# An adaLN block with a Mamba-2 scan: last weights staged in eight buffers, and the loads around them in another order

## The chip, the cores and the metric

One core of a Trainium2 chip runs the whole program. The metric is the device time of one execution in microseconds, lower is better. Everything is fp32; the large products are made of three TensorE passes over split operands (a high part in the reduced format fp32r and the low remainder).

## The reference, cut to what matters

```python
mod = (silu(c) @ wmod).reshape(4, 6, 1, 512)               # sa, ca, ga, sb, cb, gb
h = layernorm(x) * (1 + ca) + sa                            # x: 4 x 512 x 512
xBCzA = h @ in_proj_w.T                                     # x 1024, B 512, C 512, z 1024, A 64
xBC = silu(causal_depthwise_conv4(xBCzA[..., :2048]) + bias)
y = ssd_chunk_scan(x, -softplus(A), B, C, 128) + D * x / dt # 64 heads of 16, 8 groups of state 64
out = (y * silu(z + z_bias)) @ out_proj_w.T                 # 1024 -> 512
x = x + ga * out
h = layernorm(x) * (1 + cb) + sb
bw = where(w >= 0, 1, -1) * mean(|w|, axis=1)               # binarized ffn weight, 512 x 512
return x + gb * (h @ bw.T + b_ffn)
```

## The kernel before, in words

The program has three parts. A prologue makes the modulation, the normalized input `h_hi`/`h_lo` (4 batches, resident in SBUF) and the decays of all heads, which go to scratch tensors in DRAM. The main part and the tail follow in one block; each engine's instruction stream is written out by hand, and engines meet only at semaphores.

**The main part** has 16 steps (4 pairs of groups `gp` times 4 batches `b`), each of 4 units of 128 tokens, so 64 units, v = 0 to 63; every engine runs over v = -2 to 63, and a unit has four slots (`sl`). In a unit TensorE multiplies states and diagonal blocks (L1023, L1036, L1049), the Gram matrix (L1061), turns x and B (L1003, L1013), multiplies decays (L994) and makes one and a half tiles of the input projection, 12 matmuls of 128x512 each, for a step ahead (L985). ScalarE evicts the tiles, takes tanh and exp; VectorE makes the convolution taps (L1223), the silu (L1245, L1250), the product `mix` (L1259), `update` and `collect` (L1289, L1273, L1275); GpSimd makes the state decay and finishes y, step by step, in `t1`. The SP queue issues all DMAs in program order and waits itself: in each unit it waits until the decay product of unit v+2 is done, then loads the decays of unit v+4 (`R`, `Lm`); at the first unit of a step it first waits for GpSimd's y of the step before (L917), stores it (L918) and loads the scales `ea` (L893); at the third unit it loads the skips `dd`.

**Weights** come in raw, 128 rows of 512, are turned by TensorE in two pieces (`weights(i)`, L1074, a piece is 2 transposes; piece 2j is in slot 3 of a unit, piece 2j+1 in slot 0 of the next), evicted by ScalarE (L1166 to L1170), and their low part is made on GpSimd. Two raw buffers `wraw` alternate. For the next group pair, six blocks (pieces 0 to 11): blocks 0 and 1 are loaded at (b, i) = (0, 3), the others at (2, 0) to (2, 3), each behind what SP does in that unit; block 2 is turned in slot 3 of the group's unit 9, that is (2, 1). For the tail, twelve blocks j: 0 to 7 of the output projection, 8 to 11 of the ffn weight; block j is loaded by SP in unit 49+j (`OUT_UNIT` - 1 + j) and turned in units 50+j and 51+j. Before an ffn block is turned, ScalarE takes its absolute value (`magnitudes`, L1176, slot 3 of units 57 to 60), and VectorE its mean and its signs in place (`signs`, L1295 to L1302, slot 1 of units 58 to 61). `alpha` (L1084), a product of ones with the means, follows in unit 63.

**The tail** has 16 steps (batch, block of 128 rows), numbered n = 0 to 15. For each: y loaded from scratch (`load_tail_y`, 512 KB), x loaded (256 KB), ScalarE's `high_y` (L1523), GpSimd's `low_y` (L1562), 24 matmuls (L1683, `project`), `residual` on VectorE (L1613 to L1621: times gate `ga`, plus x, statistics), the reciprocal deviation on GpSimd (L1577 to L1581), `normalize` (L1532) on ScalarE, four transposes (L1698, `turn`), scale and shift (L1547, L1553), the low part (`split`, L1637), 8 matmuls (L1713, `linear`) and `finish` (L1650, L1653). Projections 0 and 1 already run in slots of units 61 to 63 (`TAIL_AT`). Project(n+2) needs low_y(n+2), which needs high_y(n+2), which stands behind normalize(n) on ScalarE. SP in unit 59 loads y of blocks 0, 1 and x of blocks 0 to 3; in unit 62 it waits for the last input projection and the last decay product, and then loads gates 0, the ffn bias, y of blocks 2, 3 and the other gates. GpSimd's `shift(b)` (L1572) multiplies the bias by gate `gb` of batch b: shift(0) before its tail starts, and shift(1) to shift(3) in steps 0 to 2; VectorE's `scale_gates(b)` (L1628) in steps 0 to 3. After unit 63 VectorE runs residual(0), then finishes the last y of the main part (L1336, L1339), which SP stores (`store_last`) before its later tail loads.

Of the kernel before, what the change touches and what calls it, by code (L numbers as in the profile page):

```python
# [10 lines left out]
P = 128  # L11
# [134 lines left out]
def early_tail(nc, s, ctx):  # L146
# [7 lines left out]
    s.y_hi, s.y_lo = sb("y_hi", [P, 2, DI // P, P], F32R), sb("y_lo", [P, 2, DI // P, P], F32R)  # L154
# [5 lines left out]
    s.d_gate, s.d_bias = [sem(f"d_gate{b}") for b in range(NB)], sem("d_bias")  # L160
# [625 lines left out]

TAIL_AT = {246: (0, 0), 247: (0, 1), 249: (0, 2), 250: (0, 3), 251: (1, 0), 253: (1, 1), 254: (1, 2), 255: (1, 3)}


def main_part(nc, s, outer, x, w_in, w_out, w_ffn, b_ffn):  # L790

    with ExitStack() as ctx:
# [47 lines left out]
        def chunk(u, c):  # L840
            first = (u % UPS) * U_TOK + c * Q
            return slice(first, first + Q)

# [23 lines left out]
        def sync(sp, tail):  # L867
# [41 lines left out]
            def load_last_weights(j):  # L909

                r, hh = j % 4, j // 4
                src = w_out[r * P:(r + 1) * P, hh * D:(hh + 1) * D] if hh < 2 else w_ffn[r * P:(r + 1) * P, :]
                sp.wait_ge(w_pe, NWP + 2 * (j - 2) + 2)
                sp.dma_start(wraw[:, j % 2, :], src).then_inc(wraw_ready[j % 2], 16)
# [12 lines left out]
            for v in range(-2, NU):  # L927
# [12 lines left out]
                if v >= 0 and n // NB < GP - 1:  # L940
# [4 lines left out]
                    if (b, i) in ((2, 0), (2, 1), (2, 2), (2, 3)):  # L945
                        load_weights(gp + 1, i + 2)

                if 0 <= v - OUT_UNIT + 1 < (NWO + NWF) // 2:
                    load_last_weights(v - OUT_UNIT + 1)
                if v == 59:  # L950
# [7 lines left out]
                if v == 62:  # L958

                    sp.wait_ge(in_done, len(TILES))  # L960
                    sp.wait_ge(d_done, 2 * NU)
                    load_gates(s, sp, 0)
                    sp.dma_start(s.bias, b_ffn.rearrange("(o n) -> o n", o=1).broadcast_to([P, D])).then_inc(s.d_bias, 16)
                    for t in range(2, 4):
                        load_tail_y(nc, s, sp, 0, t)
                    for b in range(1, NB):
                        load_gates(s, sp, b)
# [6 lines left out]
        def tensor(pe, tail):  # L974
# [90 lines left out]
            def weights(i):  # L1065

                raw, half = i // 2, i % 2
                if half == 0:
                    pe.wait_ge(wraw_ready[raw % 2], 16 * (raw // 2 + 1))
                    if i >= NWP + NWO:  # L1070
                        pe.wait_ge(s.w_sign, (i - NWP - NWO) // 2 + 1)
                wait(pe, w_copied, i)
                for k in range(2):
                    ins = pe.transpose(XT[:, k * P:(k + 1) * P], wraw[:, raw % 2, (2 * half + k) * P:(2 * half + k + 1) * P],  # L1074
                                       s.ident[:, :])
# [48 lines left out]
        def scalar(act, tail):  # L1124
# [47 lines left out]
            def magnitudes(r):  # L1172

                act.wait_ge(wraw_ready[r % 2], 16 * ((NWP + NWO) // 4 + r // 2 + 1))
# [585 lines left out]
```

## Time and profile before

| | |
|---|---|
| median of 3 runs | 780.71 us (777.64 to 781.13) |
| the profiled execution | 776.95 us, its span 775.1 us |
| mean granted TensorE clock | 0.929 of full speed |
| busy: TensorE, VectorE, ScalarE, GpSimd | 681.3, 523.3, 377.8, 384.4 us |
| DMA moved | 71.55 MB, mean 92 GB/s |

The profile records one execution. All times in rows are microseconds from the start of the span. 1.85 us of the profiled execution lie outside its span. "Idle before" is time in which an engine had nothing to run, and the name behind it is what ended that time; "issue" stands where the profile saw no engine that did, which is also what a wait for a DMA can look like on TensorE.

### The profile page before, as it was taken

The page shows a single profiled execution, that of the slowest core. Times are in us where ns is not written, and L with a number is a line of the kernel's source. Part 1 is how long each engine was busy: PE and PEld are TensorE (multiplying, and loading weights), DVE is VectorE, ACT ScalarE, POOL GpSimd, SP SyncE. Part 2 cuts the span into 40 slices and gives each one's busy share as a digit, 9 for nine tenths or more (in the row PEclk, how much of TensorE's full clock was granted, in tenths as well). Part 3 has the DMA queues.
Part 4 walks back from the last instruction along what each step waited for, and adds up shares of the span by engine and source line. Part 5 has one row for each costly group of instructions (what it writes and reads, how often), then busy time and mean ns, then how long its engine had stood idle before and what let it go on. Part 6 is the DMA issues. An engine that isn't in the chain of part 4 may idle for free. (4 is left out here: it accounts for less than half of the span.)

```text
span 775.1 us, 20785 instructions
## 1 busy us (share of the span) xinstructions
PE 681.3 (88%) x8194; PEld 533.1 (69%) x8194; DVE 523.3 (68%) x940; ACT 377.8 (49%) x812; POOL 384.4 (50%) x465
## 2 busy tenths in 40 slices
PE   6678348999989999989999989999875797999995
PEld 6457116777767777767777767777664575788883
DVE  2759576878857777758778777687572454665643
ACT  0562413455554644555554554655562425565653
POOL 2674800144535435446345364456471547776761
PEclk9666579999999999999999999999997799999998
DMA  7440352111132022123123123122322563535311
GB/s 199 110 163 28 135 189 60 35 60 63 62 98 77 33 88 89 33 94 107 35 68 108 34 86 98 53 74 75 112 88 61 166 163 124 155 117 156 118 41 41
DMA packets 61909, 71.55 MB, mean 92 GB/s; under 512 B 13992, under 2 KB 32936, under 8 KB 61812
## 3 DMA queue, kind: packets, MB, share of 16 engines
q1 hardware_dynamic: 56372, 70.17, 28.5%
q8 instruction: 66, 1.08, 0.6%
q10 hardware_dynamic: 5440, 0.05, 0.4%
q14 instruction: 31, 0.25, 0.1%
HBM read 54.45 MB, written 15.75 MB: 91 GB/s over the span
## 5 line engine op out<-in xcount | busy, mean ns | idle before, releaser
L1223 DVE SCALAR_TENSOR_TENSOR m_cv<-bank,gpc,m_cv 128x511 f32<-128x511 f32 (+2 forms) x192 | 143.6, 748 | 54.1 <-ACT m_cv L1132 49.5
L985 PE MATMUL bank<-h_hi,w_hi 128*128 128x512 f32 x384 | 159.1, 414 | 12.6 <-DVE m_Xp L1305 11.5
L985 PE MATMUL bank<-h_hi,w_lo 128*128 128x512 f32 x384 | 152.2, 396 | 0.0
L985 PE MATMUL bank<-h_lo,w_hi 128*128 128x512 f32 x384 | 151.6, 395 | 0.0
L1132 ACT ACTIVATE m_cv<-bank,gpc 128x512 f32<-128x512 f32 x96 | 71.9, 749 | 91.2 <-PE bank L985 91.2
L1358 POOL TENSOR_TENSOR m_S<-m_S,m_cd 128x128 f32<-128x128 f32 x96 | 39.8, 415 | 146.7 <-DVE m_S L1286 78.2
L985 PEld LDWEIGHTS bank<-h_hi,w_hi 128*128 128x128 f32 x384 | 73.3, 191 | 31.4 <-DVE m_Xp L1305 11.7
L1349 POOL TENSOR_TENSOR m_Xw<-m_Xp,wend 128x256 f32<-128x256 f32 x64 | 39.9, 624 | 110.1 <-ACT m_Xp L1152 110.1
L985 PEld LDWEIGHTS bank<-h_hi,w_lo 128*128 128x128 f32 x384 | 72.8, 190 | 16.9
L1144 ACT ACTIVATE m_M<-bank 128x512 f32<-128x512 f32 x128 | 76.3, 596 | 13.4 <-PE bank L994 11.8
L985 PEld LDWEIGHTS bank<-h_lo,w_hi 128*128 128x128 f32 x384 | 73.4, 191 | 13.7
L1259 DVE TENSOR_TENSOR m_M<-m_M,bank 128x512 f32<-128x512 f32 x128 | 81.7, 680 | 0.0
L1049 PE MATMUL pair<-m_M,m_Xp 64*32 64x64 f32 x4096 | 62.3, 229 | 0.0
L994 PE MATMUL bank<-R,Lm 84*128 84x512 f32 x128 | 58.3, 456 | 3.1 <-ACT m_M L1144 3.1
L1139 ACT ACTIVATE bank<-m_cv 128x512 f32<-128x512 f32 x96 | 58.1, 605 | 2.6 <-DVE m_cv L1223 2.6
L1250 DVE SCALAR_TENSOR_TENSOR m_gate<-bank,m_cv 128x512 f32<-128x512 f32 x32 | 22.1, 692 | 52.9 <-ACT bank L1139 52.9
L1683 PE MATMUL bank<-h_hi,t_y_hi 128*128 128x512 f32 x128 | 52.7, 411 | 3.3 <-POOL t_y_lo L1562 3.3
L1049 PEld LDWEIGHTS pair<-m_M,m_Xp 64*32 64x32 f32 x4096 | 54.6, 107 | 1.2 <-issue 0.2
L1683 PE MATMUL bank<-h_lo,t_y_hi 128*128 128x512 f32 x128 | 51.4, 402 | 0.0
L1683 PE MATMUL bank<-h_hi,t_y_lo 128*128 128x512 f32 x128 | 51.4, 401 | 0.0
L1562 POOL TENSOR_TENSOR t_y_lo<-h_lo_place,t_y_hi 128x1024 fp32r<-128x1024 f32 x16 | 38.2, 2386 | 26.3 <-ACT t_y_hi L1523 26.3
L1152 ACT ACTIVATE m_Xp<-bank 128x256 f32<-128x256 f32 x64 | 24.3, 380 | 49.0 <-PE bank L1003 49.0
(178 smaller groups left out, 1368.0 us busy)
## 6 DMA issues: line engine op xcount, KB each, us to landing
m_ea<-ea_scratch SPq DMA_DIRECT2D x32, 256.0 KB
m_dd<-dd_scratch SPq DMA_DIRECT2D x32, 256.0 KB
y_scratch<-m_t SPq DMA_DIRECT2D x16, 512.0 KB, 3.4
h_lo_place<-y_scratch SPq DMA_DIRECT2D x16, 512.0 KB, 4.3
p_wm<-in_L_wmod_dram SPq DMA_DIRECT2D x6, 1024.0 KB, 6.3
m_wraw<-in_L_attn_in_proj_w_dram SPq DMA_DIRECT2D x18, 256.0 KB, 3.3
p_xt<-in_L_attn_input__dram SPq DMA_DIRECT2D x16, 256.0 KB, 2.8
w_lo_place<-in_L_attn_input__dram SPq DMA_DIRECT2D x16, 256.0 KB, 4.5
```

Of the source, the lines that this page charges most:

```text
L985: ins = pe.matmul(A[k % 3][:, :], w[:, t, kc, :], h[:, n % NB, kc, :], start=(m == 0), stop=(m == 11))
L994: pe.matmul(DB[:, :], s.Lm[:, u % 2, q, :], s.R[:, u % 2, q, :], start=True, stop=True).then_inc(d_done, 1)
L1049: ins = pe.matmul(YS[32 * j:32 * j + 32, c, q * Q:(q + 1) * Q], Xp[half, u % 2, HG * q + h, :], M[half, u % 2, q, h * Q:(h + 1) * Q], star ...
L1132: act.activation(cv[:, k % 3, :], A[k % 3][:, :], ACT.Identity, scale=scale, bias=bias).then_inc(lin_done, 1)
L1139: act.activation(A[k % 3][:, :], cv[:, k % 3, :], ACT.Tanh).then_inc(tanh_done, 1)
L1144: act.activation(M[:, u % 2, q, :], DB[:, :], ACT.Exp).then_inc(exp_done, 1)
L1223: ins = dve.scalar_tensor_tensor(out=cv[:, k % 3, lag:], in0=A[k % 3][:, 0:L - lag], scalar=s.gpc[:, gp, o:o + 1], in1=cv[:, k % 3, lag:], ...
L1259: dve.tensor_tensor(m, m, g, ALU.mult).then_inc(m_done, 1)
L1349: pool.tensor_tensor(Xw[:, :, :].rearrange("p q (j e d) -> p (q j) e d", e=2, d=HD), src, w, ALU.mult).then_inc(xw_done, 1)
L1358: pool.tensor_tensor(S1[:, c, :].rearrange("p (h d) -> p h d", h=HG), S[:, (m - 1) % 4, :].rearrange("p (h d) -> p h d", h=HG), cd[:, gp, ...
L1562: pool.tensor_tensor(y_lo[:, st.b % 2, :, :], yt_v(st.b), y_hi[:, st.b % 2, :, :].bitcast(F32), ALU.subtract).then_inc(ylo_done, 1)
L1683: ins = pe.matmul(OB[i][:, :], y[:, i, k, :], w[k], start=(k == 0 and m == 0), stop=(k == KI - 1 and m == 2))
```

## The change

Two SBUF tensors of the tail, `y_hi` and `y_lo` (16 KB of each partition), are not used until unit 60. The change lays eight raw buffers `s.raw` in the same bytes. Blocks 0 to 9 of the last weights use them (block j in buffer (6+j) mod 8), blocks 10 and 11 use `wraw`. Each block has its own semaphore.

- Loads of last weights: blocks 0 to 7 in units 40 to 47, 10 and 11 in units 49 and 50 (after the last input weights are turned), 8 and 9 in units 53 and 54 (after blocks 0 and 1 are turned).
- `magnitudes` in slot 3 of units 55 to 58 (was 57 to 60), `signs` in slot 3 of units 56 to 59 (was slot 1 of 58 to 61). Block j is turned where it was.
- Input weights of the next group pair: blocks 2 to 5 loaded at (1, 3), (2, 0), (2, 1), (2, 2), each one unit earlier.
- First y tiles and x tiles in unit 58 (was 59). In unit 61 (was 62), behind the wait for the last projection alone: y 2, `ga` 0, y 3, bias; then, behind the wait for the last decay product, `gb` 0 and the other gates.
- residual(0) at slot 0 of unit 63, ahead of that unit's `collect`; the last y (`close`) behind residual(1). `shift(b+1)` and `scale_gates(b)` in the third step of each batch. GpSimd waits in unit 61 until block 9 is turned.

```diff
-    s.y_hi, s.y_lo = sb("y_hi", [P, 2, DI // P, P], F32R), sb("y_lo", [P, 2, DI // P, P], F32R)
+    with nc.sbuf_tensor("t_y_hi", [P, 2, DI // P, P], F32R) as s.y_hi, nc.sbuf_tensor("t_y_lo", [P, 2, DI // P, P], F32R) as s.y_lo:
+        pass
+    s.raw = sb("raw", [P, 8, D])
+    s.raw_ready = [sem(f"raw_ready{j}") for j in range((NWO + NWF) // 2)]
...
+SIGN_AT = {55: 0, 56: 1, 57: 2, 58: 3}
+LAST_WEIGHTS_AT = {**{40 + j: j for j in range(8)}, 49: 10, 50: 11, 53: 8, 54: 9}
...
+        def raw_of(j):
+
+            if j < NWO // 2 + 2:
+                return s.raw[:, (6 + j) % 8, :]
+            return wraw[:, j % 2, :]
...
-                src = w_out[r * P:(r + 1) * P, hh * D:(hh + 1) * D] if hh < 2 else w_ffn[r * P:(r + 1) * P, :]
-                sp.wait_ge(w_pe, NWP + 2 * (j - 2) + 2)
-                sp.dma_start(wraw[:, j % 2, :], src).then_inc(wraw_ready[j % 2], 16)
+                if hh < 2:
+                    src = w_out[r * P:(r + 1) * P, hh * D:(hh + 1) * D]
+                else:
+                    src = w_ffn[r * P:(r + 1) * P, :]
+                    sp.wait_ge(w_pe, NWP + 4 if r < 2 else NWP)
+                sp.dma_start(raw_of(j), src).then_inc(s.raw_ready[j], 16)
...
-                    if (b, i) in ((2, 0), (2, 1), (2, 2), (2, 3)):
-                        load_weights(gp + 1, i + 2)
-
-                if 0 <= v - OUT_UNIT + 1 < (NWO + NWF) // 2:
-                    load_last_weights(v - OUT_UNIT + 1)
-                if v == 59:
+                    if (b, i) in ((1, 3), (2, 0), (2, 1), (2, 2)):
+                        load_weights(gp + 1, 2 + (i + 1) % 4)
+
+                if v in LAST_WEIGHTS_AT:
+                    load_last_weights(LAST_WEIGHTS_AT[v])
+                if v == 58:
...
-                if v == 62:
+                if v == 61:
 
                     sp.wait_ge(in_done, len(TILES))
-                    sp.wait_ge(d_done, 2 * NU)
-                    load_gates(s, sp, 0)
+                    load_tail_y(nc, s, sp, 0, 2)
+                    load_gate(s, sp, 0, 0)
+                    load_tail_y(nc, s, sp, 0, 3)
                     sp.dma_start(s.bias, b_ffn.rearrange("(o n) -> o n", o=1).broadcast_to([P, D])).then_inc(s.d_bias, 16)
-                    for t in range(2, 4):
-                        load_tail_y(nc, s, sp, 0, t)
-                    for b in range(1, NB):
-                        load_gates(s, sp, b)
+            sp.wait_ge(d_done, 2 * NU)
+            load_gate(s, sp, 1, 0)
+            for b in range(1, NB):
+                load_gate(s, sp, 0, b)
+                load_gate(s, sp, 1, b)
...
-                act.wait_ge(wraw_ready[r % 2], 16 * ((NWP + NWO) // 4 + r // 2 + 1))
+                act.wait_ge(s.raw_ready[NWO // 2 + r], 16)
                 wait(act, s.w_stats, r)
-                act.activation(s.wabs, wraw[:, r % 2, :], ACT.Abs).then_inc(s.w_abs, 1)
+                act.activation(s.wabs, raw_of(NWO // 2 + r), ACT.Abs).then_inc(s.w_abs, 1)
...
-                    r = v - OUT_UNIT - NWO // 2
-                    if sl == 1 and 0 <= r < 4:
-                        signs(r)
-            tail.residual(dve, Step(0, 0))
+                    if sl == 3 and v - 1 in SIGN_AT:
+                        signs(SIGN_AT[v - 1])
+                    if (v, sl) == (NU - 1, 0):
+                        tail.residual(dve, Step(0, 0))
+
+        def close(dve):
+
...
                 if v in (60, 61):
+                    if v == 61:
+                        pool.wait_ge(w_pe, NWP + NWO + 4)
                     tail.low_y(pool, Step(0, v - 60))
...
+def load_gate(s, sp, g, b):
+
+    sp.dma_start((s.ga, s.gb)[g][:, b, :], s.g_d[g, b:b + 1, :].broadcast_to([P, D])).then_inc((s.d_ga, s.d_gb)[g][b], 16)
...
-            if st.gp == 0 and st.b < NB - 1:
-                shift(st.b + 1)
+            if st.b == 2 and st.gp < NB - 1:
+                shift(st.gp + 1)
...
-            if st.gp == 0:
-                scale_gates(st.b)
+            if st.n(1, 0) == 1:
+                main.close(dve)
+            if st.b == 2:
+                scale_gates(st.gp)
```

## Rows read from the trace of the kernel before

**Rows 1.** Who waited for whom, whole span: total us, times, longest

```profile
ACT t_att L1176 <- DMA m_wraw<-in_L_ffn_weight_dram: 16.9, 4, 7.0
...
PE bank L1074 <- issue: 15.6, 5, 4.8
```

**Rows 2.** Timeline of TensorE: start, length, instruction, idle time before it

```profile
218.12 0.64 PE L1074 MATMUL bank<-ident,m_wraw 128*128 128x128 f32 x2 [2.90 <-issue]
...
221.84 0.48 PE L985 MATMUL bank<-h_hi,w_hi 128*128 128x512 f32 x1
...
339.15 0.41 PE L1074 MATMUL bank<-ident,m_wraw 128*128 128x128 f32 x2 [3.07 <-issue]
...
341.50 0.47 PE L985 MATMUL bank<-h_hi,w_hi 128*128 128x512 f32 x1
...
551.88 0.78 PE L985 MATMUL bank<-h_hi,w_hi 128*128 128x512 f32 x1
...
583.26 0.66 PE L1074 MATMUL bank<-ident,m_wraw 128*128 128x128 f32 x2 [4.78 <-issue]
```

**Rows 3.** Timeline of the SP queue, first unit of a step

```profile
330.83 0.39 SPq L918 DMA_DIRECT2D y_scratch<-m_t  x1
...
334.91 0.36 SPq L907 DMA_DIRECT2D m_wraw<-in_L_attn_in_proj_w_dram  x1
```

**Rows 4.** Timeline of TensorE, first instruction of units 56, 57, 59, 60, 61 and 62

```profile
565.09 0.39 PE L1023 MATMUL pair<-m_Ct,m_S 128*128 128x128 f32 x2
...
572.36 0.61 PE L1023 MATMUL pair<-m_Ct,m_S 128*128 128x128 f32 x4
...
591.36 0.61 PE L1023 MATMUL pair<-m_Ct,m_S 128*128 128x128 f32 x4
...
605.75 0.64 PE L1023 MATMUL pair<-m_Ct,m_S 128*128 128x128 f32 x2
...
615.05 0.61 PE L1023 MATMUL pair<-m_Ct,m_S 128*128 128x128 f32 x4
...
626.80 0.61 PE L1023 MATMUL pair<-m_Ct,m_S 128*128 128x128 f32 x4
```

**Rows 5.** Timeline of VectorE, units 57, 58 and 63

```profile
575.80 1.28 DVE L1259 TENSOR_TENSOR m_M<-m_M,bank 128x512 f32<-128x512 f32 x2
...
587.41 0.69 DVE L1295 BATCH_NORM_STATS2 t_wsta<-t_att 128x6 f32<-128x512 f32 x1
...
589.51 1.27 DVE L1259 TENSOR_TENSOR m_M<-m_M,bank 128x512 f32<-128x512 f32 x2
...
635.41 0.68 DVE L1613 TENSOR_TENSOR t_att<-bank,w_hi_place 128x512 f32<-128x512 f32 x1
```

**Rows 6.** Timeline of ScalarE, start of the tail

```profile
637.07 0.60 ACT L1210 ACTIVATE w_hi_place<-bank 128x512 f32<-128x512 f32 x1 [7.51 <-PE bank L1084]
641.07 0.81 ACT L1532 ACTIVATE t_xn<-t_x,t_small 128x512 f32<-128x512 f32 x1 [3.40 <-POOL t_small L1581]
```

**Rows 7.** Timeline of TensorE, start of the tail

```profile
645.31 0.80 PE L1683 MATMUL bank<-h_hi,t_y_hi 128*128 128x512 f32 x1 [2.72 <-POOL t_y_lo L1562]
...
652.33 0.60 PE L1698 MATMUL bank<-ident,t_xn 128*128 128x128 f32 x4
...
654.61 0.39 PE L1683 MATMUL bank<-h_hi,t_y_hi 128*128 128x512 f32 x1
...
660.22 0.60 PE L1698 MATMUL bank<-ident,t_xn 128*128 128x128 f32 x4
```

**Rows 8.** Timeline of GpSimd, the two first steps of the tail

```profile
637.85 1.12 POOL L1577 TENSOR_TENSOR t_small<-t_small 128x1 f32<-128x1 f32 x1 [3.45 <-DVE t_small L1621]
...
647.70 0.18 POOL L1577 TENSOR_TENSOR t_small<-t_small 128x1 f32<-128x1 f32 x1
```

**Rows 9.** Instructions of L1428, the loads of y: time from issue to landing

```profile
DMA to landing us min/median/max: 4.1/4.3/9.9
```

More of the change, by code:

```diff
@@ L159, in early_tail @@
     s.d_x = [sem(f"d_x{t}") for t in range(4)]
-    s.d_gate, s.d_bias = [sem(f"d_gate{b}") for b in range(NB)], sem("d_bias")
+    s.d_ga, s.d_gb, s.d_bias = [sem(f"d_ga{b}") for b in range(NB)], [sem(f"d_gb{b}") for b in range(NB)], sem("d_bias")
     s.w_abs, s.w_stats, s.w_mean, s.w_diag, s.w_step, s.w_sign, s.al_pe, s.al_done = (
@@ L1067, in weights @@
                 raw, half = i // 2, i % 2
+                src = wraw[:, raw % 2, :] if i < NWP else raw_of(raw - NWP // 2)
                 if half == 0:
-                    pe.wait_ge(wraw_ready[raw % 2], 16 * (raw // 2 + 1))
-                    if i >= NWP + NWO:
+                    if i < NWP:
+                        pe.wait_ge(wraw_ready[raw % 2], 16 * (raw // 2 + 1))
+                    elif i < NWP + NWO:
+                        pe.wait_ge(s.raw_ready[raw - NWP // 2], 16)
+                    else:
                         pe.wait_ge(s.w_sign, (i - NWP - NWO) // 2 + 1)
@@ L1073, in weights @@
                 for k in range(2):
-                    ins = pe.transpose(XT[:, k * P:(k + 1) * P], wraw[:, raw % 2, (2 * half + k) * P:(2 * half + k + 1) * P],
-                                       s.ident[:, :])
+                    ins = pe.transpose(XT[:, k * P:(k + 1) * P], src[:, (2 * half + k) * P:(2 * half + k + 1) * P], s.ident[:, :])
                 ins.then_inc(w_pe, 1)
@@ L1202, in scalar @@
                         tanh(k)
-                    r = v - OUT_UNIT + 1 - NWO // 2
-                    if sl == 3 and 0 <= r < 4:
-                        magnitudes(r)
+                    if sl == 3 and v in SIGN_AT:
+                        magnitudes(SIGN_AT[v])
                     if (v, sl) in ((60, 0), (61, 0)):
@@ L1291, in signs @@
             def signs(r):
-                raw = wraw[:, r % 2, :]
+                raw = raw_of(NWO // 2 + r)
                 dve.wait_ge(s.w_abs, r + 1)
@@ L1417, in gpsimd @@
                 if v in (60, 61):
+                    if v == 61:
+                        pool.wait_ge(w_pe, NWP + NWO + 4)
                     tail.low_y(pool, Step(0, v - 60))
-        m_.store_last = store_last
+        m_.store_last, m_.close = store_last, close
         m_.sync, m_.tensor, m_.scalar, m_.vector, m_.gpsimd = sync, tensor, scalar, vector, gpsimd
@@ L1428, in load_tail_y @@
     sp.dma_start(s.yt[t].rearrange("p a (k n) -> p (a k) n", n=P), y_v[b, t]).then_inc(s.d_y[t], 16)
-def load_gates(s, sp, b):
-    sp.dma_start(s.ga[:, b, :], s.g_d[0, b:b + 1, :].broadcast_to([P, D])).then_inc(s.d_gate[b], 16)
-    sp.dma_start(s.gb[:, b, :], s.g_d[1, b:b + 1, :].broadcast_to([P, D])).then_inc(s.d_gate[b], 16)
+def load_gate(s, sp, g, b):
+    sp.dma_start((s.ga, s.gb)[g][:, b, :], s.g_d[g, b:b + 1, :].broadcast_to([P, D])).then_inc((s.d_ga, s.d_gb)[g][b], 16)
 def load_tail_x(nc, s, sp, x, b, t):
@@ L1566, in shift @@
         def shift(b):
-            pool.wait_ge(s.d_gate[b], 32)
+            pool.wait_ge(s.d_gb[b], 16)
             if b == 0:
@@ L1608, in residual @@
         dve.wait_ge(s.d_x[st.b], st.gp * 16 + 16)
-        dve.wait_ge(s.d_gate[st.gp], 32)
+        dve.wait_ge(s.d_ga[st.gp], 16)
         if st.n(1, 0) == 1:
```

## The prediction

> **What bounds the kernel now.** TensorE is busy for 88% of the span, so I first looked for the time in which it is not, by listing who waited for whom over the whole span. Two rows stand out that belong to the same thing: TensorE waited five times, 15.6 us in all, in front of the turning of raw weights, and ScalarE four times, 16.9 us, for the raw ffn weights themselves [rows 1]. I then read TensorE's timeline around each of the five. Outside of them the main part shows next to no gap on TensorE, so a microsecond taken from one of these waits is a microsecond of the whole; a wait of another engine counts only where TensorE stands behind it.
>
> The waits have one shape. At the first unit of a step SP stands until GpSimd has the last step's y, and only behind that store and the scales and decays does it issue the next weight block: stored at 330.83, weights at 334.91 [rows 3], while TensorE was ready for them some 3.1 us before 339.15 [rows 2]. So the block landed 4.2 us after its issue, and TensorE had stood since 336. This repeats once per group pair and twice in the output weights. A second cost follows some of them: behind an idle stretch the granted clock drops from 2.4 to 1.2 GHz and the same instructions take longer. From the turning to the next projection matmul it is 2.35 us at full clock (339.15 to 341.50) and 3.72 us at 218.12 to 221.84 [rows 2], a loss of 1.4 us. The turning at 583.26 took 0.66 instead of 0.41 us, and the matmul at 551.88 took 0.78 instead of 0.47 [rows 2]: two more such losses.
>
> **Part 1: input weights a unit earlier.** Nothing is added; three of the five waits are of this kind. The load now comes in the unit ahead of the store, when SP has just issued the decays, and waits only until the buffer's last piece is turned, in slot 0 of the next unit, some two microseconds later. It is then issued about 10 us earlier than at 334.91, and needs 4.2. The block behind it takes its old place at 334.9, and is turned a unit (7.27 us, 565.09 to 572.36 [rows 4]) later than the first: at least 3 us in hand. What stands behind SP's new wait are the next scales and store, which wait for GpSimd anyway. The fourth wait is the output block of the first step's unit 52; its new load is 9 units ahead.
> These four are worth 15.6 - 4.78 = 10.8 us [rows 1, 2] and two clock losses, 1.4 and (less, since only its end was slow) 1.2: **13.4 us**. Bounds: 10.8 if the clock losses came anyway; 0 if another wait stood right behind. TensorE's near gapless work elsewhere speaks against the latter.
>
> **Part 2: units 57 to 61.** Here the fifth wait (4.78 us at 583.26) is followed by ScalarE's waits for ffn blocks, the longest 7.0 us [rows 1], during which it can't evict the pieces that TensorE waits for. I cost this by units.
> - Unit 58 starts 4.78 earlier and has no slow clock, 1.4 less. But `signs` is now in units 56 and 57, which have convolutions. One takes 2.1 us of VectorE (587.41 to 589.51), and `mix` at 575.80 shows no idle time ahead of it, so it moves to 577.9 and ends at 579.2 [rows 5]. Behind it a silu (an estimate of 1.3, two halves of about half a `mix`) and 0.69 of statistics reach 581.2, and `magnitudes` of the next block waits for them, 0.6, then the copies of the turned piece, 0.6: 582.4. TensorE wants that at 583.26 - 4.78 + 2.15 = 580.6 (the second piece is turned 0.2 ahead of the projection, so 2.35 - 0.2 behind the first). So a new wait of 1.8; I take 1.5, since one `signs` without contention is nearer to 1.7. Bounds 0 and 4.2 (two full `signs`). Unit 59 starts 4.7 us earlier.
> - Unit 59 took 14.39 us (591.36 to 605.75) [rows 4]. It has no projection. Unit 56 has 18 matmuls of the kind of which 24 take 5.61 us (654.61 to 660.22 [rows 7]), 4.2 in all, which leaves TensorE 3.0 us of other work: the lower bound. The upper one is 14.39 - 7.0 = 7.4. Between them VectorE decides: 2.1 of `signs`, 1.3 of `mix` and, an estimate, 2.0 of updates, collect and one silu, 5.4 us. That saves 9.0.
> - Units 60 and 61 have 18 such matmuls as unit 56 has, and took 9.30 and 11.75 us [rows 4]. At 7.4 each they save 1.9 and 4.35. The last ffn block and the y tiles (loaded a unit earlier) are then there in time.
>
> Sum: 4.7 + 9.0 + 1.9 + 4.35 = **20.0 us**, with bounds of 15.3 and 22.4. The loads themselves, twelve of 0.4 us on SP and 256 KB each, cost nothing: they lie beside units in which SP waits for TensorE. GpSimd's new wait in unit 61 is for a piece turned in unit 60, so nothing too.
>
> **Part 3: start of the tail.** residual(0) ran at 635.41 [rows 5], though its projection was done some 3.5 us before. Now it is ahead of `collect`. What is late next is ScalarE, which stands at the copy of `alpha` until 637.67, so normalize(0) moves from 641.07 to 637.7 [rows 6]. From there to project(2) is 4.24 us as before (645.31 [rows 7]), through high_y and low_y: 641.9, 3.4 earlier. Its 24 matmuls took 7.02 us at the slow clock against 5.61 later [rows 7]; 1.4 more, if the shorter gap leaves the clock alone. Project(3) is then ready at 649.8, but its low_y waits for the reciprocal of step 1 on GpSimd, normalize and high_y; I estimate 650.5 for it, twice the 4.24 us behind 641.9. It was at 654.61. I take **4.3 us**, bounds 0 and 4.8. The gates: `ga` 0 is issued about 3 us earlier than before. In a queue as full as this a 512 KB load took up to 9.9 us [rows 9]; with that residual(0) would come at 633, still early. Where `bias` or `gb` 0 are as late, GpSimd's shift(0) holds the reciprocal and part 3 loses up to all. The shifts and scalings that are spread over the batches are the same work and lie beside TensorE's.
>
> `close` now stands behind residual(1), beside GpSimd's small operations of step 1 instead of step 0. Beside it the first of them took 1.12 us in step 0, and 0.18 in step 1 [rows 8]. The Trainium skill, "GPSIMD Engine Reference", section Specifications, says that GpSimd's SBUF interfaces are shared with VectorE and contend with its instructions of two SBUF inputs, which `close` has. By that rule project(3) comes 0.9 us later than without contention and part 3 gives 3.4, by the row's place in step 0 alone it gives 4.3.
>
> **The sum.** 13.4 + 20.0 + 4.3 = 37.7 us. The profiled execution took 776.95, so it would take 739.2. The median of the runs is 780.71, 3.8 us above it, so I predict 780.7 - 37.7 = **743 us**. About 0.5% (4 us) is what this measurement can tell from no change.
>
> **Rivals.**
> - *The wait moves to VectorE (0.15).* `signs`, `magnitudes` and the next `signs` wait for each other in turn, and each stands in a unit of the full schedule. For it: no idle time ahead of `mix` [rows 5]. Against it: unit 58 has no convolution to come. If each of the three later ones costs its 2.1 us on TensorE, that is 6.3, and one clock loss of 1.4: 751 us.
> - *The tail's start gains nothing (0.10).* Bias and gate 0 land late, or project(2) and (3) wait for GpSimd as before. For it: the DMA queue is full there and a load took 9.9 us [rows 9]. 743 + 4.3 = 747 us.
> - *The change doesn't do what it says in the input weights (0.05).* If what TensorE waited for was not the load (the row says "issue" and names no DMA), or a new wait on SP takes its place, 13.4 us stay: 756 us. Against it: the landing time of 4.2 us fits.
> - *Contention of VectorE and GpSimd (0.05).* The second instance of it delays project(3) by 0.9: 744 us.
> - *Slower than before (0.02).* The decays stand in the same queue as the weights. They are issued nearly two units, some 14 us, before their use. If weight blocks ahead of them held them longer than that, TensorE would wait in each of some 24 units with such a load. To be slower than 784 it must eat 41.6 us, 1.7 a unit, so landing would have to take 16 us; the longest seen is 9.9 [rows 9].
>
> **The numbers.** My case as summed has 0.60, and for itself 738 to 748. With the first two rivals and the contention that is 0.90; something smaller that I don't see has 0.03 either way. The range of 736 to 755 leaves out the third and fifth rival and half of the unseen. Faster by over 0.5% in all cases but the last and the worst of the unseen: 0.96; within 0.5% 0.02; slower 0.02.
>
> **What would show it.** Right: no wait over 1 us in front of L1074; no row of L1176 waiting for a DMA; unit 59 under 7 us; project(2) within 2.5 us behind turn(0); a clock near 0.94 or above. Wrong: a wait of TensorE for L1166 to L1170 behind L1176 waiting for L1295 (first rival); L1572 waiting for a DMA past 634 less the shift (second); L1074 still at "issue" (third); L994 waiting (fifth).

## The result, and the profile after

The changed kernel takes 748.07 us (median of 4 runs, 746.02 to 748.24) where the kernel before takes 780.92 (median of 4, 777.64 to 781.92): ratio 0.9607, 95% interval 0.9578 to 0.9635 (recorded from the single runs; the two medians alone would give 0.958). The prediction was 743 us, range 736 to 755. The profiled execution took 748.24 us, its span is 746.5 and the mean granted clock 0.944 (before: 776.95, 775.1 and 0.929). Span against span the change gives 28.6 us, where the steps of the prediction promised 37.7.

The page of the profile after: busy times of the engines, TensorE in 40 slices, and its granted clock in the same slices.

```profile
PE 674.1 (90%) x8194; PEld 527.1 (71%) x8194; DVE 536.5 (72%) x940; ACT 376.5 (50%) x812; POOL 389.4 (52%) x465
...
PE   6679256899999999999999999999998999999995
...
PEclk9757577999999999999999999999999999999997
```

From the eighth slice to the last but one TensorE is at 80% or more. Its busy time was 681.3 us before; the same number of instructions now takes 7 us less, which fits the higher mean clock.

Who waited for whom after, whole span:

```profile
PE bank L1707 <- POOL t_y_lo L1584: 7.0, 5, 1.5
...
PEld bank L1094 <- issue: 5.7, 28, 0.4
```

And one row of the same list of the kernel before:

```profile
PE bank L1683 <- POOL t_y_lo L1562: 3.3, 2, 2.7
```

The five waits in front of the turning of raw weights [rows 1] are gone (L1094 is L1074 of before), and so is ScalarE's wait for the ffn blocks. One row has grown: TensorE waits five times, 7.0 us in all, for `low_y` of GpSimd (L1584, before L1562) in the tail, where it waited twice, 3.3 us, before. The waits at project(2) and (5) were there before, with 2.72 and 0.63 us; they are 1.52 and 1.38 now, and those at project(3), (9) and (13) are new.

Busy times after in units 56 to 61, cut at the starts of the units, which answer to [rows 4]. Columns: stretch, its length, busy us (and instructions) of TensorE, weight loads, VectorE, ScalarE and GpSimd, granted clock, DMA share, GB/s:

```profile
552.27:560.01 7.74, 7.50 (x119) 5.75 (x118) 5.61 (x12) 5.80 (x14) 4.08 (x6) 1.00 0.01 4
560.01:568.11 8.10, 5.42 (x109) 4.04 (x108) 7.96 (x16) 4.78 (x12) 4.79 (x8) 0.98 0.42 131
568.11:575.34 7.23, 7.23 (x106) 5.62 (x106) 7.09 (x14) 3.78 (x10) 4.64 (x6) 0.78 0.06 12
575.34:581.06 5.72, 4.08 (x103) 2.86 (x102) 4.63 (x13) 3.65 (x10) 1.61 (x4) 1.00 0.42 130
581.06:589.79 8.73, 8.42 (x120) 6.69 (x118) 5.08 (x12) 4.27 (x10) 7.00 (x8) 0.80 0.75 227
589.79:597.23 7.44, 7.44 (x122) 6.03 (x121) 3.27 (x8) 5.41 (x12) 4.64 (x6) 1.00 0.53 161
```

Unit 59, which took 14.39 us, takes 5.72. In unit 57 VectorE is full (7.96 of 8.10) and TensorE is not; units 58 and 60 run in part at the slow clock, 0.78 and 0.80.

The same view in four stretches, cut at the starts of units 56 and 62, turn(1) and turn(15):

```profile
552.27:597.23 44.96, 40.09 (x669) 30.98 (x668) 33.63 (x71) 27.68 (x63) 26.76 (x34) 0.92 0.38 114
597.23:617.98 20.75, 19.23 (x221) 14.90 (x219) 13.05 (x19) 6.43 (x15) 12.71 (x13) 1.00 0.61 185
617.98:733.62 115.64, 107.08 (x482) 84.41 (x481) 77.32 (x102) 63.83 (x139) 86.32 (x73) 1.00 0.36 109
733.62:746.50 12.88, 6.69 (x20) 4.59 (x20) 3.37 (x5) 2.90 (x8) 0.32 (x1) 0.69 0.11 41
```

The same four stretches of the kernel before:

```profile
565.09:626.80 61.71, 43.89 (x668) 33.27 (x667) 30.33 (x71) 27.91 (x63) 27.84 (x35) 0.81 0.33 99
626.80:652.33 25.53, 20.71 (x222) 15.99 (x221) 12.17 (x21) 7.34 (x15) 13.88 (x14) 0.93 0.77 214
652.33:761.56 109.23, 105.53 (x481) 84.98 (x480) 66.81 (x100) 63.47 (x138) 79.50 (x72) 1.00 0.35 107
761.56:775.10 13.54, 7.40 (x20) 5.18 (x20) 3.37 (x5) 2.90 (x8) 0.33 (x1) 0.75 0.10 39
```

The whole difference lies in these rows. Unit 1 of the main part started at 143.14 before and at 144.36 after, in a prologue that the change does not touch; over all kernels below it lay between 142.3 and 145.0, so the first 1 or 2 us of any difference here mean nothing. I therefore count from there.

| stretch | before | after | difference | foretold |
|---|---|---|---|---|
| prologue, to unit 1 | 143.14 | 144.36 | +1.2 | 0 |
| unit 1 to unit 56 | 421.95 | 407.91 | -14.0 | -13.4 |
| unit 56 to unit 62 | 61.71 | 44.96 | -16.75 | -20.0 |
| unit 62 to turn(1) | 25.53 | 20.75 | -4.8 | -4.3 (to the whole tail) |
| turn(1) to turn(15) | 109.23 | 115.64 | +6.4 | 0 |
| turn(15) to the end | 13.54 | 12.88 | -0.7 | 0 |
| sum | 775.1 | 746.5 | -28.6 | -37.7 |

The fifth line is the surprise. The turns of `xn` in the tail came every 7.9 us before, but for 7.98 and 8.8 at turn(3) and turn(4). (From turn(0) to turn(1) it was 10.4 us, which is in the line above.) After, TensorE's timeline at projections 3, 5 and 9:

```profile
621.86 0.50 PE L1707 MATMUL bank<-h_hi,t_y_hi 128*128 128x512 f32 x1 [1.37 <-POOL t_y_lo L1584]
...
639.38 0.50 PE L1707 MATMUL bank<-h_hi,t_y_hi 128*128 128x512 f32 x1 [1.38 <-POOL t_y_lo L1584]
...
672.97 0.51 PE L1707 MATMUL bank<-h_hi,t_y_hi 128*128 128x512 f32 x1 [1.38 <-POOL t_y_lo L1584]
```

The first comes behind `close`; the others, with a like one at 706.57, behind the shifts of steps 2, 6 and 10. A step with such a wait takes 9.6 us, and the step ahead of the two last ones 8.2.

### The profile page after: what moved, and what is told of

The parts are those of the page before. It is cut to its first block and busy times, and to the rows that moved or that the text cites. A ratio compares the mean times of both kernels' runs of the same rounds, so it can differ in the third digit from the quotient of the medians.

```text
span 746.5 us, 20781 instructions
## 1 busy us (share of the span) xinstructions
PE 674.1 (90%) x8194; PEld 527.1 (71%) x8194; DVE 536.5 (72%) x940; ACT 376.5 (50%) x812; POOL 389.4 (52%) x465
## 3 DMA queue, kind: packets, MB, share of 16 engines
q8 instruction: 65, 1.06, 0.6%
## 5 line engine op out<-in xcount | busy, mean ns | idle before, releaser
L1379 POOL TENSOR_TENSOR m_S<-m_S,m_cd 128x128 f32<-128x128 f32 x96 | 39.7, 414 | 141.0 <-DVE m_S L1304 71.4
L1584 POOL TENSOR_TENSOR t_y_lo<-h_lo_place,t_y_hi 128x1024 fp32r<-128x1024 f32 x16 | 40.1, 2504 | 27.3 <-ACT t_y_hi L1545 27.3
```

The source lines that it names most:

```text
L1379: pool.tensor_tensor(S1[:, c, :].rearrange("p (h d) -> p h d", h=HG), S[:, (m - 1) % 4, :].rearrange("p (h d) -> p h d", h=HG), cd[:, gp, ...
L1584: pool.tensor_tensor(y_lo[:, st.b % 2, :, :], yt_v(st.b), y_hi[:, st.b % 2, :, :].bitcast(F32), ALU.subtract).then_inc(ylo_done, 1)
```

## The experiments

All ratios are to the kernel before, timed beside it on the same chip. "Units" is unit 56 to unit 62, "tail" is unit 62 to turn(15), both from the profiled execution, one for each kernel.

| kernel | median us | ratio, 95% interval | units | tail |
|---|---|---|---|---|
| before | 780.92 | 1 | 61.71 | 134.76 |
| after | 748.07 | 0.9607 (0.9578 to 0.9635) | 44.96 | 136.39 |
| 1 input weights only | 765.34 | 0.9851 (0.9821 to 0.988) | 59.71 | 134.76 |
| 2 shifts back | 745.99 | 0.9611 (0.958 to 0.9642) | 44.97 | 133.15 |
| 3 `close` back | 748.59 | 0.9631 (0.9591 to 0.967) | 45.04 | 135.08 |
| 4 shift ahead of low_y | 743.42 | 0.9572 (0.9543 to 0.9602) | 44.97 | 131.37 |
| 5 3 and 4 together | 741.6 | 0.9535 (0.9503 to 0.9567) | 44.83 | 130.18 |
| 6 and the sum ahead | 739.99 | 0.952 (0.9485 to 0.9556) | 45.03 | 129.70 |
| 7 signs as before | 748.47 | 0.9624 (0.9589 to 0.9659) | 44.13 | 136.39 |
| 8 signs one unit later | 746.19 | 0.9599 (0.9567 to 0.9631) | 42.77 | 136.42 |
| 9 6 and 8 together | 738.97 | 0.949 (0.9464 to 0.9515) | 41.94 | 129.64 |
| 10 9, y ahead of skips | 739.83 | 0.9501 (0.9475 to 0.9527) | 41.51 | 129.71 |
| 11 residual(0) back | 750.21 | 0.9635 (0.9606 to 0.9665) | 44.81 | 138.23 |

Among the kernels with the early loads a stretch that the edit does not touch repeats within 0.25 us (units 44.81 to 45.04, tail 136.39 to 136.42), so the two right columns tell apart what the whole times cannot. That does not hold where TensorE waits for late loads: experiment 1 changes nothing in units 56 to 61, and they took 59.71 us there and 61.71 in the kernel before, 1.2 of the 2.0 in unit 59. The gain of that stretch is thus known to 2 us only. The kernel before was timed anew three times, with medians of 776.94 (beside 1 to 4), 778.17 (5 to 8) and 778.65 us (9 to 11).

**1. Input weights only**, on the kernel before.

```diff
-                    if (b, i) in ((2, 0), (2, 1), (2, 2), (2, 3)):
-                        load_weights(gp + 1, i + 2)
+                    if (b, i) in ((1, 3), (2, 0), (2, 1), (2, 2)):
+                        load_weights(gp + 1, 2 + (i + 1) % 4)
```

> The kernel before, with input weight blocks 2 to 5 loaded one unit earlier and nothing else changed. Theory of the prediction: the three waits of 2.90, 3.07 and 2.47 us are for these loads, one with a clock loss of 1.4: 9.8 us faster than before, near 771. Rival: part of the gain of the first four waits comes from elsewhere, or a new wait on SP's w_pe takes some back: less than 7 us.

Measured: ratio 0.9851, a gain of 1.5% with the whole interval below 1, and unit 50 starts 10.3 us earlier, counted from unit 1. The waits for which nothing was changed are still there (L1074 of before, TensorE's timeline):

```profile
539.36 0.41 PE L1074 MATMUL bank<-ident,m_wraw 128*128 128x128 f32 x2 [2.56 <-issue]
...
573.89 0.66 PE L1074 MATMUL bank<-ident,m_wraw 128*128 128x128 f32 x2 [4.59 <-issue]
```

So three of the five rows named "issue" were the late load, as read from its landing time, and nothing took their place. The output block's wait (2.56 here) and the 4.59 of the last stage belong to the last weights. The third rival of the prediction, that it was not these loads, has fallen.

**2. Shifts and scalings back** in the first steps.

```diff
-            if st.b == 2 and st.gp < NB - 1:
-                shift(st.gp + 1)
+            if st.gp == 0 and st.b < NB - 1:
+                shift(st.b + 1)
...
-            if st.b == 2:
-                scale_gates(st.gp)
+            if st.gp == 0:
+                scale_gates(st.b)
```

> The changed kernel, with shift(1) to shift(3) back in steps 0 to 2 and scale_gates(0) to (3) back in steps 0 to 3. In the changed kernel turn follows turn in the tail after 7.9 us, but after 9.6 us in the steps behind each shift (627.58 to 635.51 is 7.9, 635.51 to 645.11 is 9.6), and TensorE waits there 1.38 us for low_y. Theory A: a shift (1.3 us) lengthens GpSimd's chain (reciprocal, low_y, sum), on which TensorE stands; three shifts spread cost 3 x 1.7 = 5.1 us, three in a row while the chain is still filling cost some 3 us, so this kernel is 2 to 3 us faster than the changed one (near 745.5) and has no 9.6 us step behind step 5. Rival B: the shifts are beside TensorE's work as predicted, and the 9.6 us steps come from something else (loads of the next batch): the steps stay and the time is 748. Rival C: the early gates land late and this waits at the start: slower than 748 by more than 2.

Measured: from step 5 on every step takes 7.9 us again; the first four take 9.38, 9.13, 8.37 and 8.81. Unit 62 to turn(1) is longer, 22.3 instead of 20.75 us, turn(1) to turn(15) shorter, 110.9 instead of 115.6. Together the tail is 3.2 us shorter than after. Spreading the shifts and scalings was thus a loss of 3.2 us, net of what it spares at the start; the ratio of the whole (0.9611) is too coarse to show it beside after's.

**3. `close` back**, ahead of residual(1).

```diff
+            if st.n(1, 0) == 1:
+                main.close(dve)
             if not is_first(st):
                 residual(dve, st)
...
-            if st.n(1, 0) == 1:
-                main.close(dve)
```

> The changed kernel, with the last y (close) ahead of residual(1) again. In the changed kernel the two small operations of GpSimd in step 1 took 1.17 and 1.60 us beside close (0.19 and 0.57 in step 0), and TensorE waited 1.37 us for low_y(3) at 621.86. Contention theory: beside step 0, where ScalarE stands at the copy of alpha anyway, they cost nothing; project(3) comes 1.4 to 1.7 us earlier, time near 746.5. Rival: low_y(3) is late for another reason (its own chain), then it stays at 621.9 or residual(1), now behind close, makes it later: 748 or above.

Measured: the second step takes 7.9 instead of 9.6 us and the tail 1.3 us less. GpSimd's first two operations of step 1, after and then here (its timeline; L1599 and L1601 work on one element per partition):

```profile
613.86 1.17 POOL L1599 TENSOR_TENSOR t_small<-t_small 128x1 f32<-128x1 f32 x1
615.11 1.60 POOL L1601 TENSOR_TENSOR t_small<-t_small 128x1 f32<-128x1 f32 x1
```

```profile
614.77 0.64 POOL L1599 TENSOR_TENSOR t_small<-t_small 128x1 f32<-128x1 f32 x1
615.49 0.55 POOL L1601 TENSOR_TENSOR t_small<-t_small 128x1 f32<-128x1 f32 x1
```

After, VectorE ran `close` from 613.62 to 616.3, over both of them. They took 2.8 us, here 1.2. The contention rival of the prediction is what happens, and larger than the 0.9 us given for it. The tail gains less than the 1.7 us of the second step, since the step to turn(3) takes 8.35 us here and 7.93 after. The Trainium skill, "GPSIMD Engine Reference", section Specifications, says that GpSimd's SBUF interfaces contend with VectorE's instructions of two SBUF inputs. These numbers agree: both instructions of `close` have two such inputs. No run changes only the number of inputs, so the rule itself is not tested here.

**4. The shift ahead of low_y**, in the same steps as in the change.

```diff
+            if st.b == 2 and st.gp < NB - 1:
+                shift(st.gp + 1)
             if two_more(st):
                 low_y(pool, st.next().next())
...
-            if st.b == 2 and st.gp < NB - 1:
-                shift(st.gp + 1)
```

> The changed kernel, with shift(b+1) in the same step (the third of a batch) but ahead of low_y instead of behind the sum. GpSimd is idle for 1.88 us there in each step, while ScalarE runs normalize and high_y. Theory A (chain): the 1.3 us of a shift go into that idle time, the three 9.6 us steps become 7.9, and the kernel is 4.5 to 5.5 us faster than the changed one, near 743. Rival B (work beside VectorE's is what costs, wherever it stands) or a late high_y: the steps stay near 9.6 and the time is 748.

Measured: the three steps of 9.6 us behind a shift are down to 7.9, that of `close` stays, and the tail is 5.0 us shorter, ratio 0.9572. The same instructions run, only their order differs. This experiment shows the mechanism best, by its stretches; its interval still overlaps after's. GpSimd's timeline of a step with a shift, after:

```profile
627.31 2.41 POOL L1584 TENSOR_TENSOR t_y_lo<-h_lo_place,t_y_hi 128x1024 fp32r<-128x1024 f32 x1 [1.88 <-ACT t_y_hi L1545]
629.67 1.75 POOL L1614 TENSOR_TENSOR t_f<-t_x,t_gbias 128x512 f32<-128x512 f32 x1
631.38 1.31 POOL L1594 TENSOR_TENSOR t_gbias<-gb,w_hi_place 128x512 f32<-128x512 f32 x1
632.65 0.64 POOL L1599 TENSOR_TENSOR t_small<-t_small 128x1 f32<-128x1 f32 x1
633.37 0.88 POOL L1601 TENSOR_TENSOR t_small<-t_small 128x1 f32<-128x1 f32 x1
634.35 0.26 POOL L1603 TENSOR_SCALAR t_small<-t_small 128x1 f32<-128x1 f32 x1
636.49 2.84 POOL L1584 TENSOR_TENSOR t_y_lo<-h_lo_place,t_y_hi 128x1024 fp32r<-128x1024 f32 x1 [1.88 <-ACT t_y_hi L1545]
```

and with the shift ahead:

```profile
624.60 1.31 POOL L1594 TENSOR_TENSOR t_gbias<-gb,w_hi_place 128x512 f32<-128x512 f32 x1
626.51 2.39 POOL L1584 TENSOR_TENSOR t_y_lo<-h_lo_place,t_y_hi 128x1024 fp32r<-128x1024 f32 x1 [0.60 <-ACT t_y_hi L1545]
628.86 1.75 POOL L1616 TENSOR_TENSOR t_f<-t_x,t_gbias 128x512 f32<-128x512 f32 x1
630.57 0.19 POOL L1599 TENSOR_TENSOR t_small<-t_small 128x1 f32<-128x1 f32 x1
...
634.28 2.41 POOL L1584 TENSOR_TENSOR t_y_lo<-h_lo_place,t_y_hi 128x1024 fp32r<-128x1024 f32 x1 [1.88 <-ACT t_y_hi L1545]
```

Without a shift one low_y follows the last by 7.77 us (626.51 to 634.28). In that loop GpSimd works 5.9 us and waits 1.88 for normalize and high_y, which ScalarE can only begin when GpSimd's reciprocal is there. TensorE's step is 7.90. The loop has 0.13 us of room in each step, so a shift of 1.31 us put between two low_y eats what ten steps save, and with the slower small operations behind it the loop took 9.18 (627.31 to 636.49). The low_y at its end also took 2.84 us instead of 2.41, which makes the 9.6 us from one projection to the next. In the 1.88 us in which GpSimd waits anyway, it costs nothing.

**5. Both**, `close` back and the shift ahead.

> The changed kernel with both edits of the tail that took a wait away: shift(b+1) ahead of low_y, and close ahead of residual(1). If they act on different waits (the three behind shifts, 1.7 each, and the one behind close, 1.3), they add up: turns 7.9 us apart throughout, 6 to 6.5 us below the changed kernel. If the wait behind close only moves the point from which GpSimd's chain is late, less than 5.5.

Measured: tail 130.18, that is 6.2 us less than after; the single edits gave 1.3 and 5.0. They add up. Ratio 0.9535, whose interval lies wholly below after's. The tail now is 4.6 us below before's, close to the 4.3 foretold for part 3.

**6. The sum too.** The addition of the shift (L1614 of after), which stood between low_y and the next reciprocal, goes ahead of low_y, and the shift behind low_y.

```diff
+            pool.tensor_tensor(f1[:, st.b % 2, :], x2[:, st.b, :], gbias[:, st.gp, :], ALU.add).then_inc(res_done, 1)
             if two_more(st):
                 low_y(pool, st.next().next())
+            if st.b == 2 and st.gp < NB - 1:
+                shift(st.gp + 1)
```

> As the kernel with close and shift moved, but here the sum x2 + gbias (1.3 to 1.75 us) stands ahead of low_y, in the 1.88 us in which GpSimd waits for high_y, and the shift behind low_y. Chain theory: GpSimd's chain is shortened by up to 1.7 us in every step, so the shift behind low_y costs nothing either, and also the small waits of 0.3 us go: as the kernel with close and shift moved or up to 1 us less. Rival: the sum waits for finish of two steps before, and delays low_y: waits of 0.5 us and more in each step, 5 us more.

Measured: the tail is 0.5 us shorter (129.70), all its steps take 7.9 to 8.2 us. GpSimd waits there 0.62 us for high_y and 1.58 for VectorE's statistics, so its work now leaves room in the loop, and a step with a shift behind low_y takes 8.1 us at most. The ratio, 0.952, cannot be told from that of 5.

**7 and 8. Where `signs` stand.** First in the units of before, slot 1; then in slot 3, one unit later than in the change.

```diff
-SIGN_AT = {55: 0, 56: 1, 57: 2, 58: 3}
+SIGN_AT = {57: 0, 58: 1, 59: 2, 60: 3}
...
-                    if sl == 3 and v - 1 in SIGN_AT:
+                    if sl == 1 and v - 1 in SIGN_AT:
```

```diff
-SIGN_AT = {55: 0, 56: 1, 57: 2, 58: 3}
+SIGN_AT = {56: 0, 57: 1, 58: 2, 59: 3}
```

> The changed kernel, with the early loads but magnitudes and signs where they were before (slot 3 of units 57 to 60, slot 1 of units 58 to 61). In the changed kernel units 56 and 57 last 7.74 and 8.10 us (7.27 for unit 56 before), with waits of TensorE of 1.08 and 1.59 us in unit 57 and a slow clock behind them. Theory S: the signs among the convolutions cause them; here units 56 and 57 take 7.3 and about 6.6, the block's copy waits nowhere for a load, units 58 to 61 grow by at most 1 in all, and the time is 2 to 3 us below the changed kernel. Rival: the light units 58 to 61 then carry signs in line with magnitudes and the copy of the piece, and lose as much as 56 and 57 gain: time as the changed kernel within 1.

> The changed kernel, with magnitudes and signs one unit later (slot 3 of units 56 to 59 and of 57 to 60). Theory S: unit 56 is back at 7.3 (0.45 less); unit 57 still has the signs behind its silu, so part of its waits stays, and signs(0) is used for the piece in slot 3 of unit 58 in time: 1 to 2 us below the changed kernel. Rival: TensorE now waits for the signs themselves in slot 3 of units 58 to 61, as block and signs are one unit apart: no faster or slower by up to 2.

Measured, units 56 to 61, one by one:

| | 56 | 57 | 58 | 59 | 60 | 61 | sum |
|---|---|---|---|---|---|---|---|
| before | 7.27 | 11.36 | 7.64 | 14.39 | 9.30 | 11.75 | 61.71 |
| after | 7.74 | 8.10 | 7.23 | 5.72 | 8.73 | 7.44 | 44.96 |
| 7 as before | 7.28 | 6.18 | 6.70 | 7.72 | 7.90 | 8.35 | 44.13 |
| 8 one later | 7.26 | 6.17 | 7.30 | 5.79 | 8.82 | 7.43 | 42.77 |

With the signs where they were, units 56 to 58 take 20.16 us, 6.1 less than before, all three at a clock of 1.00: the 4.78 + 1.4 that the prediction gave the load alone. After, they take 23.07, so the signs among the convolutions cost 2.9 us, where I had taken 1.5. But as before they make units 59 and 61 longer, with TensorE waiting 1.92 us for `mix` at 579.88, so the rival is nearer to what came. The wait of 1.08 us in unit 57, which the expectation gave to the signs, is not theirs: it is there in 7 and 8 too, and with 1.09 in the kernel before. One unit later is best: 2.2 us less than after. The whole times of 7 and 8 do not differ from after's by more than their intervals.

**9. Best of these**, 6 with the signs of 8.

> The kernel with close and the sum moved, and with magnitudes and signs one unit later. Units 56 to 61 took 44.96 us in the changed kernel and 42.77 with the signs one unit later; the tail's moves took 6.7 to 7.5 us out between turn(1) and turn(15). Theory: the two lie in different stretches and add up, 8.9 to 9.7 us below the changed kernel, near 738.5. Rival: the earlier start of unit 62 meets gates and y tiles that are not there, and the start of the tail gives it back: near 740.5.

Measured: units 41.94, tail 129.64, together 9.8 us less than after: the two add up. The ratio is 0.949, and its interval (0.9464 to 0.9515) lies below after's, so it beats both kernels. Its median is 39.7 us below the kernel before's.

**10. y ahead of the skips.** In unit 58 the loads of y 0 and 1 are issued before the skips.

> As the kernel before it in this set, with the two first y tiles issued in unit 58 ahead of the skips (two loads of 256 KB) instead of behind them. ScalarE waited 1.73 us for the first y tile in unit 60 of the changed kernel, and TensorE 1.2 us behind that with the signs later, with a slow clock after it. Theory: the tile comes 1.2 us and more earlier, unit 60 goes from 8.8 to at most 7.6 us, time 1 us or a little more below. Rival: the wait before it, for the last projection of step 14, sets the issue, and the skips come late for GpSimd: no gain.

Measured: unit 60 takes 7.52 instead of 7.95 us; the time of the whole shows no gain, as the rival said. ScalarE's wait for y 0 is thus real and, here, small.

**11. residual(0) back** behind the unit loop, all else as after.

```diff
-                    if (v, sl) == (NU - 1, 0):
-                        tail.residual(dve, Step(0, 0))
...
+            tail.residual(dve, Step(0, 0))
+
         def close(dve):
```

> The changed kernel with residual(0) behind unit 63 as before. Theory of the prediction: residual(0) starts 2.9 us later (605.3 instead of 602.4), but ScalarE stands at the copy of alpha until 608.1 anyway, so normalize(0) and project(2) come only 1.2 to 1.5 us later, 1.2 to 2.5 us above the changed kernel with the clock. Rival: the whole gain of 4.8 us at turn(1) hangs on this move, then turn(1) comes 3.5 to 5 us later.

Measured: turn(1) comes 24.0 us behind unit 62 (after 20.75, before 25.53), but it then waits for nothing at project(3), so the tail as a whole is 1.8 us longer than after's. ScalarE's timeline here:

```profile
607.07 0.60 ACT L1228 ACTIVATE w_hi_place<-bank 128x512 f32<-128x512 f32 x1 [7.52 <-PE bank L1103]
609.08 0.81 ACT L1553 ACTIVATE t_xn<-t_x,t_small 128x512 f32<-128x512 f32 x1 [1.42 <-POOL t_small L1602]
```

xn starts 2.0 us behind the copy of `alpha`. Before, it was 4.0 [rows 6], with residual(0) at the same place. What differs is that `close` no longer stands beside GpSimd's reciprocal of step 0: its three operations took 1.12, 1.62 and 0.27 us before, 3.0 in all, and here 0.19, 0.57 and 0.27. After, xn(0) follows the copy at once, at 608.00, as the prediction had it.

Experiment 3 is the other half of this comparison: residual(0) moved, and `close` beside step 0 as before. ScalarE's timeline there:

```profile
608.42 0.60 ACT L1228 ACTIVATE w_hi_place<-bank 128x512 f32<-128x512 f32 x1 [7.52 <-PE bank L1103]
608.91 0.81 ACT L1554 ACTIVATE t_xn<-t_x,t_small 128x512 f32<-128x512 f32 x1
```

| from unit 62 to | xn(0) | turn(1) |
|---|---|---|
| before | 14.3 | 25.5 |
| only `close` moved (11) | 12.3 | 24.0 |
| only residual(0) moved (3) | 10.8 | 20.7 |
| both (after) | 10.8 | 20.75 |

So residual(0) alone gives the whole 3.5 us at xn(0) and 4.8 at turn(1), as the prediction had it: the reciprocal is then done before the copy of `alpha` ends, contention or not. The move of `close` gives 2.0 only where residual(0) is late. With residual(0) moved too, it gives nothing at the start and costs 1.3 in the tail (experiment 3). The expectation's 1.2 to 2.5 us for the whole came true (1.8 in the tail), but turn(1) came 3.3 us later, nearly what its rival said.

## Why the prediction was right, and where it was not

The signs that the prediction named for being right all came: no wait over 1 us in front of L1094, no wait of L1195 (before L1176) for a DMA, unit 59 at 5.72 us, project(2) 2.1 us behind turn(0), a clock of 0.944. They test the loads and the start of the tail, and none of them looks at the tail's later steps, where it went wrong.

**Part 1, 13.4 us: 14.0.** The four waits and both clock losses are gone and nothing stood behind them; experiment 1 shows three of them alone (10.3, where their share of the sum was 9.8). No wait of TensorE took their place: L1094 shows none above 0.4 us.

**Part 2, 20.0 us: 16.75** (14.75 against the trace of experiment 1, which has the same late loads). The loads are what it hung on, and two of the four terms are right: unit 59 gave 8.7 (9.0 foretold) and unit 61 4.3 (4.35). The two others were mis-sized. (The bounds given for the part, 15.3 and 22.4, do not follow from those of its terms, which add up to 15.2 and 23.8.)
- To the start of unit 59: 3.2 instead of 4.7. I priced the signs among convolutions at 1.5, experiment 7 measures 2.9. The wait is where the prediction put it. TensorE's timeline at the end of unit 57:

```profile
567.60 0.33 PE L1029 MATMUL bank<-ident,m_Bt 128*128 128x128 f32 x1 [1.59 <-DVE m_M L1277]
567.76 0.55 PE L1094 MATMUL bank<-ident,t_raw 128*128 128x128 f32 x2
568.11 1.06 PE L1039 MATMUL pair<-m_Ct,m_S 128*128 128x128 f32 x4
```

  The 1.59 is the new wait for `mix`. What I had left out is behind it: the last row took 1.06 us where its kind takes 0.61, and the granted clock is 0.50 from 568.1 to 570.0: the short wait also brought slow clock. And one `signs` took 2.8 us, not 2.1, since its in-place step at 560.86 took 1.55 us beside a GpSimd multiplication, where it had taken 0.83.
- Unit 60: 0.6 instead of 1.9. TensorE is busy there for 8.42 of 8.73 us at a clock of 0.80: it is slow clock again, behind the light unit 59. Kernels in which unit 60 ran at a clock of 1.00 show a second cost that lay hidden under it: in 8 ScalarE stood 2.43 us for y 0 and TensorE 1.22 us behind it (8.82 us in all), in 9 it was 1.57 and 0.36 (7.95), in 10, with y issued earlier, 1.14 and none (7.52). So the 7.4 that I gave the unit is about what it takes with neither.

**Part 3, 4.3 us: a loss of 1.6**, outside its bounds of 0 and 4.8. Its start was as foretold: 4.8 us at turn(1), by the move of residual(0) (experiments 3 and 11). **The step that failed is the sentence that the spread shifts and scalings "are the same work and lie beside TensorE's".** They lie beside TensorE's work, but not beside GpSimd's own loop, and that is as long as TensorE's. The place of the shifts cost 5.0 us, 1.7 for each (experiment 4), the contention behind `close` 1.3 (experiment 3). Before, shift(1) and shift(2) stood where project(2) and (3) were late anyway, and shift(3) cost about 0.9 there: the step to turn(4) took 8.8 us.

The steps of 8.2 us stay in experiments 4 and 5 and are gone in 2. No run moves the scalings alone, but the traces point at them. VectorE's timeline after, ahead of such a step, and then GpSimd's:

```profile
656.07 0.84 DVE L1650 TENSOR_TENSOR gb<-gb,w_hi_place 128x512 f32<-128x512 f32 x1
...
657.67 0.69 DVE L1675 TENSOR_TENSOR t_o<-t_o,t_f 128x512 f32<-128x512 f32 x1
```

```profile
657.69 1.33 POOL L1603 TENSOR_SCALAR t_small<-t_small 128x1 f32<-128x1 f32 x1
```

The scaling pushes VectorE's additions of `finish` onto the last operation of GpSimd's reciprocal, which takes 1.33 us there and 0.26 to 1.06 in the other steps. The 1.33 stands behind scalings in the traces of 3, 4 and 5 too, and nowhere in that of 2. A scaling so costs some 0.3 us, as far as the traces can show it.

I could have read it. The row of the kernel before for turn(1) to turn(15) has GpSimd busy for 79.5 us, and in the list of waits of that stretch it waits 24.5 us for high_y:

```profile
POOL t_y_lo L1562 <- ACT t_y_hi L1523: 24.5, 13, 1.9
POOL t_small L1577 <- DVE t_small L1621: 4.7, 1, 4.7
ACT t_xn L1532 <- POOL t_small L1581: 23.9, 14, 3.2
```

79.5 + 24.5 + 4.7 = 108.7 of 109.23 us. That busy time and waits fill a stretch says nothing by itself; what counts is who ended the waits. The 24.5 us are for high_y, which stands behind normalize on ScalarE, and that in turn waits for GpSimd's reciprocal (the third row). So nearly all of GpSimd's idle time belongs to its own loop; only the 4.7, in the last step, is a wait for others. Being busy for 73% hid that. The loop can be timed directly, in GpSimd's timeline of the kernel before:

```profile
676.60 2.40 POOL L1562 TENSOR_TENSOR t_y_lo<-h_lo_place,t_y_hi 128x1024 fp32r<-128x1024 f32 x1 [1.88 <-ACT t_y_hi L1523]
...
684.37 2.40 POOL L1562 TENSOR_TENSOR t_y_lo<-h_lo_place,t_y_hi 128x1024 fp32r<-128x1024 f32 x1 [1.88 <-ACT t_y_hi L1523]
```

It takes 7.77 us where TensorE's step takes 7.9.

**The rivals.** *The wait moves to VectorE* came half true: one wait of 1.59 us with slow clock, not three. *Contention* is true and part of the loss. *The tail gains nothing* came near in its number, 747, by coincidence: part 3 lost 5.9 us and not 4.3, and the mechanism was none of its two, not a late gate, not project(2), but the steps behind them. The slower case did not come: no unit waits for the decays.

**The balance.** 37.7 foretold less 3.3 (part 2), 5.9 (part 3) and 1.2 (the prologue), plus 0.6 (part 1) and 0.7 (the end), is 28.6. The medians, 780.92 and 748.07, are 32.9 us apart, so against them the error is smaller, 743 for 748.07: the profiled execution of before was faster than all four of these runs. That is luck of the starting point. The later medians of the kernel before, 777 to 779 us, less 37.7 would give 739 to 741. And 748.07 is just outside the 738 to 748 that the case as summed had for itself.

## What to carry to other kernels

An engine off the critical path can still be full: add its busy time to the waits that are part of its own loop, and compare that with the step of the engine that sets the pace. Where they are equal, a microsecond of "hidden" work costs at least one (here 1.3 us of work cost 1.7), and its place in the loop decides: the same shift costs 1.7 us behind low_y and nothing in the wait ahead of it. And a load that was issued too late was worth its whole wait plus the slow clock behind it. Moving it by one unit cost nothing here: SP waits 2.6 us at most for its buffer, and TensorE not at all.

## What the runs showed of the hardware that was not expected

- An operation of GpSimd on one element per partition took 0.19 us alone and 1.17 beside a VectorE instruction of two SBUF inputs and 1024 elements; the next one 0.57 and 1.60. It goes the other way too: VectorE's in-place `signs` step of 512 elements took 1.55 us beside GpSimd's multiplication (560.86 after), and 0.39 where GpSimd did nothing (575.61 after).
- The clock fell not only behind a stall. Behind unit 59, where TensorE works 4.1 of 5.7 us and waits never more than 0.73 us at a time, unit 60 ran at 0.80 after and at 1.00 in experiment 9. TensorE's instructions in these two units are the same in both, but not what came before: after had slow clock in unit 58 too (0.78), experiment 9 had none. A microsecond hangs on it.
